# Attention of the picked rows in a graph and feed-forward network: context products in two halves, the mix's last rows added tile by tile

## The reference, cut to what matters

```
normed = _ln(hidden_states, g1, b1)
scores = sigmoid(normed @ Wr + br)
_, idx = top_k(-scores, k)                    # k = 188 rows of 1250 are picked
q, kk, v = normed @ Wq + bq, normed @ Wk + bk, normed @ Wv + bv     # 12 heads of 64
probs = softmax(q @ kk^T / sqrt(64))
ctx = probs @ v
attn_out = ctx @ Wo + bo
pooled = sum(w * normed)                      # w = scores / (sum(scores) + 1e-6)
mix_out = (normed + scores * pooled) @ Wm + bm
merged = where(picked, attn_out, mix_out)
h = hidden_states + merged
n2 = _ln(h, g2, b2)
return h + gelu(n2 @ W1 + bf1) @ W2 + bf2
```

## Time and profile before

| what | value |
| --- | --- |
| time, median of 3 runs | 3018.88 us |
| lowest and highest | 3018.45 and 3022.26 us |
| the profiled execution's own time | 3013.21 us |
| its span | 3011.5 us |
| PE busy | 2577.1 us (86%) |
| PEld busy | 2053.6 us (68%) |
| DVE busy | 2083.0 us (69%) |
| ACT busy | 1282.9 us (43%) |
| POOL busy | 313.8 us (10%) |
| mean granted clock of PE | 0.913 |

### The profile page before, as it was taken

How to read it: one execution, slowest core, us unless ns; L and a number is a source line. 1 busy time by engine, 2 the same in 40 slices (tenths; PEclk the granted TensorE clock), 3 DMA queues, 4 the chain that set the end, 5 groups by cost and what they waited for, 6 DMA issues and landing times. The chain is left out here.

```text
span 3011.5 us, 36877 instructions
## 1 busy us (share of the span) xinstructions
PE 2577.1 (86%) x13464; PEld 2053.6 (68%) x13465; DVE 2083.0 (69%) x3004; ACT 1282.9 (43%) x1560; POOL 313.8 (10%) x160
## 2 busy tenths in 40 slices
PE   7887894888854994799999999699999989897989
PEld 3556891323322994455699999599888769896768
DVE  6775899999963554599288889560467688235655
ACT  1573226988920000111477777222565563222511
POOL 0000000000003895000000000251000000000013
PEclk9997556999975997899999999899999999998989
DMA  2467443511005554542555643362534352312003
GB/s 68 135 181 174 149 144 114 194 35 51 17 32 160 199 194 133 211 173 95 162 162 169 179 117 106 111 198 79 179 120 130 99 180 94 84 48 64 1 26 93
DMA packets 165812, 366.01 MB, mean 122 GB/s; under 512 B 29390, under 2 KB 89628, under 8 KB 164769
## 3 DMA queue, kind: packets, MB, share of 16 engines
q1 hardware_dynamic: 120728, 274.54, 30.3%
q10 hardware_dynamic: 35968, 73.97, 6.9%
q0 software_dynamic: 8960, 15.41, 2.0%
HBM read 280.88 MB, written 82.93 MB: 121 GB/s over the span
## 5 line engine op out<-in xcount | busy, mean ns | idle before, releaser
L1593 PE MATMUL gat_acc<-far_u,gat_ft 125*65 125x512 f32 x720 | 286.8, 539 | 57.7 <-DVE far_u L1661 57.3
L1593 PEld LDWEIGHTS gat_acc<-far_u,gat_ft 125*65 125x65 f32 x720 | 93.9, 142 | 246.9 <-issue 154.2
L1053 PE MATMUL rg_out<-rg_w,rg_hT 128*125 128x384 f32 x720 | 234.3, 489 | 0.0
L2183 PE MATMUL rg2a_acc<-rg2a_value_part,rg2a_wts_part 125*125 125x512 f32 x600 | 205.0, 342 | 14.8 <-DVE rg2a_wts_part L1902 11.4
L2184 PE MATMUL rg2a_acc<-rg2a_value_part,rg2a_wts_part 125*125 125x512 f32 x600 | 205.6, 343 | 0.0
L2185 PE MATMUL rg2a_acc<-rg2a_value_part,rg2a_wts_part 125*125 125x512 f32 x600 | 204.1, 340 | 0.0
L1053 PEld LDWEIGHTS rg_out<-rg_w,rg_hT 128*125 128x125 f32 x720 | 135.7, 189 | 97.5 <-issue 1.8
L1628 ACT ACTIVATE far_u<-gat_rows,gat_ks 125x1250 f32<-125x1250 f32 x118 | 156.8, 1329 | 43.1 <-PE gat_acc L1593 34.1
L1641 DVE TENSOR_TENSOR far_u<-far_u,gat_lowb 125x1250 f32<-125x1250 f32 x120 | 174.4, 1454 | 0.4 <-PEq L701 0.4
L1661 DVE SCALAR_TENSOR_TENSOR far_u<-far_u,counts_u 125x1250 f32<-125x1250 f32 x120 | 174.4, 1454 | 0.0
L370 PE MATMUL sums<-src_hot,key_hot 125*125 125x512 bf16 (+1 forms) x618 | 139.4, 355 | 27.0 <-DVE key_hot L305 25.5
(11 more groups left out here) (530 smaller groups left out, 6434.1 us busy)
## 6 DMA issues: line engine op xcount, KB each, us to landing
rg2a_values<-values_dram SPq DMA_DIRECT2D x89, 384.0 KB, 3.3
rg1a_counts<-counts_dram SPq DMA_DIRECT2D x26, 820.3 KB
rg_mask<-far_dram SPq DMA_DIRECT2D x60, 312.5 KB, 3.6
moe_raw<-in_L_ffn_w SPq DMA_DIRECT2D x16, 1152.0 KB, 5.7
relw_chunk<-in_L_gnn_W ACTq DMA_DIRECT2D x36, 384.0 KB, 3.1
gat_rows<-rows_dram SPq DMA_DIRECT2D x10, 1250.0 KB, 5.7
sorted_dram<-gat_zeros SPq DMA_DIRECT2D x30, 384.0 KB, 9.0
values_dram<-rg_stage ACTq DMA_DIRECT2D x30, 384.0 KB, 2.3
```

The lines of the kernel that those rows point to most:

```text
L1053: last = pe.matmul(self.out_ps[n % 2][:, a, 0:384], self.hT[:, c, t * TP:(t + 1) * TP], self.w_sb[r % 2][:, c, a * 384:(a + 1) * 384], sta ...
L1593: last = pe.matmul(acc[h % 2][0:WIDTH, b, 0:c1 - c0], ft[:, t, h, :], wts[i % HB][:, c0:c1], start=(t == 0), stop=(t == NT - 1))
L2183: pe.matmul(out, still[0], moving[0], start=first, stop=False)
```

## The change

Three things are moved, and no arithmetic is added or removed.

1. `context(i)` becomes two halves of five products. PE's order for a pair is now turn, half a context, turn, half a context, and so on. The waits of the context stay ahead of its first half, its signal `ctx_made` behind the second.
2. The four bias products with `bo` are taken ahead: two before the last unit's context, two behind it. The wait for DVE's last taking of a context stands behind them.
3. In the third mix piece the rows are added tile by tile: from tile 5 on, behind the taking of each product, the rows of two tiles are added. The first two pieces stay as they were.

```diff
@@ keys_and_mix, DVE
-            def add_rows(m):
+            def both_parts(m):
 
                 dve.wait_ge(row_in, 32 * (m + 1))
+                link(dve.tensor_tensor(extra[0:TP, 0, :], extra[0:TP, 0, :], extra[0:TP, 1, :], op=ALU.add))
+
+            def add_rows(m, t):
+
                 cols = slice(m * PIECE, (m + 1) * PIECE)
-                link(dve.tensor_tensor(extra[0:TP, 0, :], extra[0:TP, 0, :], extra[0:TP, 1, :], op=ALU.add))
-                for t in range(NT):
-                    link(dve.scalar_tensor_tensor(out=z[:, t, cols], in0=extra[0:TP, 0, :], scalar=keep[:, 1, t:t + 1],
-                                                  in1=z[:, t, cols], op0=ALU.mult, op1=ALU.add))
-                    last = dve.scalar_tensor_tensor(out=z[:, t, cols], in0=extra[0:TP, 2, :], scalar=keep[:, 0, t:t + 1],
-                                                    in1=z[:, t, cols], op0=ALU.mult, op1=ALU.add)
-                last.then_inc(row_used, 1)
+                link(dve.scalar_tensor_tensor(out=z[:, t, cols], in0=extra[0:TP, 0, :], scalar=keep[:, 1, t:t + 1],
+                                              in1=z[:, t, cols], op0=ALU.mult, op1=ALU.add))
+                return dve.scalar_tensor_tensor(out=z[:, t, cols], in0=extra[0:TP, 2, :], scalar=keep[:, 0, t:t + 1],
+                                                in1=z[:, t, cols], op0=ALU.mult, op1=ALU.add)
...
-                if t == NT - 1:
-                    dve.wait_ge(dve_took, n + 1)
-                    add_rows(m)
+                if m < PIECES - 1:
+                    if t == NT - 1:
+                        dve.wait_ge(dve_took, n + 1)
+                        both_parts(m)
+                        for u in range(NT):
+                            last = add_rows(m, u)
+                        last.then_inc(row_used, 1)
+                elif t >= 5:
+                    if t == 5:
+                        both_parts(m)
+                    for u in (2 * t - 10, 2 * t - 9):
+                        dve.wait_ge(dve_took, n - t + u + 1)
+                        last = add_rows(m, u)
+                    if t == NT - 1:
+                        last.then_inc(row_used, 1)
@@ attend_picked, PE
-            def context(i):
+            def context(i, half):
                 q, h = units[i]
                 at = slice(h % 2 * DH, h % 2 * DH + DH)
-                pe.wait_ge(turned_out, 2 * i + 2)
-                if i:
-                    pe.wait_ge(ctx_out, i)
-                for t in range(NT):
+                if half == 0:
+                    pe.wait_ge(turned_out, 2 * i + 2)
+                    if i:
+                        pe.wait_ge(ctx_out, i)
+                for t in range(5 * half, 5 * half + 5):
                     last = pe.matmul(ctx_ps[at, 0:QT], v[:, t, h * DH:(h + 1) * DH],
                                      probsT[i % 2][:, t, :], start=(t == 0), stop=(t == NT - 1))
-                last.then_inc(ctx_made, 1)
+                if half == 1:
+                    last.then_inc(ctx_made, 1)
+
+            def bias(q):
+                for a in range(2):
+                    cols = slice(a * 384, (a + 1) * 384)
+                    pe.matmul(score_ps[q][0:QT, a, 0:384], ones[:, :], bo_row[:, cols], start=True, stop=False)
 
             scores(0)
             for i in range(len(units)):
                 if i % 2 == 0 and i + 2 < len(units):
                     scores(i // 2 + 1)
-                turn(i, 0)
-                if i:
-                    context(i - 1)
-                turn(i, 1)
-            context(len(units) - 1)
-            pe.wait_ge(ctx_out, len(units))
+                for half in range(2):
+                    turn(i, half)
+                    if i:
+                        context(i - 1, half)
             pe.wait_ge(wo_in, 16)
             pe.wait_ge(small_in, 32)
             pe.wait_ge(one_set, 1)
+            bias(0)
+            for half in range(2):
+                context(len(units) - 1, half)
+            bias(1)
+            pe.wait_ge(ctx_out, len(units))
             for q in range(2):
                 for a in range(2):
                     cols = slice(a * 384, (a + 1) * 384)
-                    pe.matmul(score_ps[q][0:QT, a, 0:384], ones[:, :], bo_row[:, cols], start=True, stop=False)
                     for c in range(KC):
```

## The result

The changed kernel is slower. Over 20 runs each, its median is 3043.01 us (3021.61 to 3054.99) against 3019.59 (3014.77 to 3025.45); the ratio is 1.0073, 95% interval 1.0058 to 1.0089. On the 3018.88 of the prediction that ratio makes 3040.9, inside the range of 3021 to 3042 near its upper end; the bare median lies 1 us above it. The direction and the mechanisms were as forecast. The size was +22 us by the ratio in place of +12.6.

The account below looks back on a forecast made before the run. The prediction took the chain through DVE and ACT, as long as PE's 9.50 us period, as the bound. Terms -5.8 - 1.0 + 14.5 - 1.1 + 6.0 = +12.6 on 3013.21 gave 3025.8, plus 5.7 to the median: 3031.5, range 3021 to 3042.

Parts of the forecast that it names:

- What bounds the kernel: Loop over pairs: the chain through PE, DVE and ACT is as long as the 9.50 us period, without slack.
- Mix, -5.8: End of the mix: ACT's copy at 2740.72 becomes last, against 2746.54, -5.8 us; bound -4.6 with rows landing late.
- First scores, -1.0: First scores after the mix: shorter idleness may keep the clock up; bounds 0 and -2.1 us, middle taken.
- Loop, +14.5: Loop over pairs: half a turn 0.71 and half a context 0.90 join the chain, period 11.11, nine periods +14.5 us.
- Last pair and end, -1.1: Last pair to end of the products with Wo: -1.1 us, of which early biases filling two waits give 1.07.
- Clock, +6.0: Loop: PE idles some 1.8 us in one piece, clock falls in four of ten pairs, 1.5 us each.
- The faster one: Rival, loop: taking a context doesn't hold the second maximum, halves fill 0.74 us per pair; 3003 us, chance 0.08.
- No falls of the clock, 3025.5: Rival, loop: it lengthens but the clock stays up, 3018.88 + 6.6 us; chance 0.25.

Follow-up runs that it names:

- e3: Changed kernel with DVE's taking of the context moved behind the pair's second maximum; 3006.25 us, ratio to before 0.9946.
- e8: Changed kernel with ACT's two exponentials of a pair one copy later, DVE's order left; 3001.44 us, ratio to before 0.9941.
- e9: Changed kernel profiled once more, nothing altered; 3035.55 us (one).
- e5: Changed kernel with four unread products more per pair in PE's idle piece before turn(a+1, 1); 3027.79 us, ratio to before 1.0023.
- e4: Changed kernel with DVE's taking behind the second maximum and ACT's two exponentials of a pair one copy later; 3000.17 us, ratio to before 0.9933.
- e1: Changed kernel with the contexts whole again between the two turns; 3007.95 us, ratio to before 0.9956.
- e2: Kernel before with the contexts in halves and nothing else; 3054.31 us, ratio to before 1.0106.
- e6: Kernel before with only the third mix piece's rows added tile by tile; 3013.39 us, ratio to before 0.9983.
- e10: Kernel before profiled once more, nothing altered; 3026.15 us (one).
- e11: e4 with two unread products more in PE's wait ahead of the spreading stage; 3001.09 us, ratio to before 0.9926.

## Why the prediction was right, and where it was off

In the first pair of profiles the sum is +17.8 against the forecast +12.6. Of the 5.2 between them the clock makes 4.7 and the loop 1.8; the first scores and the end came out 1.4 better.

**What bounds the kernel.** Right. The chain scores, turn, context, taking, second maximum, exponential, copy, turn was the period, without slack. e3 and e8 cut it at two different links, and the period fell to 9.36 and 9.19.

**Mix, -5.8.** Right: the gap before the first scores fell from 7.96 to 2.10, 5.9 us, with the rows landing 0.23 us late, which ACT's copy hides. The bound of -4.6 doesn't follow from its rows: 2725.88 + 4.3 + 9.71 + 1.65 = 2741.54 against 2746.54 makes -5.0. Nothing hung on it.

**First scores, -1.0.** Between the bounds, as a mean of two outcomes: 2.1 in five of nine profiles, 0.6 to 0.7 in four. The gap of two microseconds keeps the clock up in some executions and not in others.

**Loop, +14.5.** Right in mechanism, 1.8 us short: 11.31 in place of 11.11 per period, 16.3 in nine. The step that was off is the half context, which I took as 0.90, half of the whole. Five products take 0.96 between turns. All three half contexts of a period that lie on the chain cost that 0.06 more: 0.17 of the 0.20.

**Last pair and end, -1.1.** The biases give 2.05 by themselves, because products of one kind in a row run shorter than those between others, which the rows of before did not show. The changed kernel's profile has 40.08 against 39.91 all the same. 1.7 us of that are the sixth fall, the scores of its last pair (4.04 in place of 2.34), and belong to the clock; the other 0.5 are the lengthened chain. Without the fall the stretch is 1.5 us shorter, near the forecast.

**Clock, +6.0.** This term was mis-sized, and it is the greatest part of the miss. I had four falls in ten pairs, 1.5 us each. The changed kernel's first profile has six, 1.6 to 1.7 each, 9.9 us in all, and another 0.84 left over from the pairs before the loop. That of e9 has seven: six in the nine periods, five of 1.6 to 1.7 and one of 2.8 (28.44 - 16.3 - 1.0 left over = 11.1), and a seventh from which the clock came back only in the products with Wo, which cost another 11 us; the forecast had nothing of that kind. So the number of falls was off more than their price. The price I had taken from the unit that stood beside a fall in the earlier trace rows, a turn and a context; in the loop it is mostly the scores of the next pair that pay, 3.5 to 4.0 us in place of 2.34. The case itself, that an idle piece of 1.8 us among short products lets the clock fall, was right, and e5 shows cause and price: the piece filled, the clock stays and 15 us come back. Why it falls behind some of these pieces and not behind others stays open.

**The rivals.** The faster one fell: the second maximum is held by the taking. It was right on one point that I had not seen as a kernel: with the taking and the exponentials out of the way, e4, the halves do fill the waits. That e4's 3000 is close to that rival's 3003 is partly luck: the ten loop pairs were to give 7.4 us and the end 2, and in e4's profile nine periods give 3.45 and the end 3.66. No falls of the clock, 3025.5: refuted by both profiles, and nearly what e5 measures with its filler (3027.79). By the Trainium skill (TensorE: Matmul & The Clock Gate, section Why this matters for your kernels) nothing should have fallen in the loop, since no idle gap in it was as long as those it warns of; the trace disagrees, with falls behind gaps of 1.88 us, so the measurement decides.

**What stays open.** The start of the first scores lies between 2732.9 and 2750.9 us in the thirteen profiles, for reasons ahead of the change, of which the mix part explains 6. That spread of executions is seen and not explained here. That medians differ by more than the first pair of profiles does is in keeping with e9, but two profiles don't give a distribution. The other way round, in e1, e3, e4 and e8 the medians gain 2 to 7 us more than the stages of their one profile add up to (e8: 11.5 by stages, 18 measured). That is not explained either, so the stages carry the argument and the medians only its direction and rough size.

## What to carry to other kernels

Before filling an idle gap of an engine, follow the wait that the filler delays. Here 0.74 us of idleness was off the chain, and the half turn put ahead of a context's last product was on it, through two other engines. When a product is moved back, look at what its consumer's engine has queued behind the consumer: a copy out that stood between two maxima, and an exponential that stood ahead of a copy, carried the 0.7 us of half a turn to PE's next turn, and with the half context ahead of the next scores, 0.96, the pair became 1.81 us longer. The same halves gave 0.55 us per pair (9.50 to 8.95) as soon as those two queues were reordered, which costs a line each. And count the clock when a wait among short products grows: behind 1.88 us of it the clock fell in six and in seven of ten pairs.

## What the runs showed of the hardware that I had not expected

The low clock can last through work without a pause. In six of twelve profiles without a filler there (e1, e2, e3, e5, e6, e10) the clock fell behind the 2.03 us wait ahead of the spreading stage and stayed at 0.50 through eighty products, though PE had no idle time in them. From e1, windows, and the row of PE:

```profile
2886.00:2890.00 4.00, 3.37 (x12) 0.64 0.02 4
2900.00:2910.00 10.00, 10.00 (x33) 0.50 0.00 0
...
2886.63 25.59 PE L3359 MATMUL att_score<-att_out,picksT 94*125 94x384 f32 x80 [2.04 <-DVE att_out L3403]
```

In the other six the same products behind the same wait took 16.5 us with the clock up. A fall there costs 8 to 9 us, in part of the executions, whether or not the kernel has the change: before has 16.50 and, in e10, 25.40; e4, e8 and both profiles of the changed kernel have 16.5, e1, e3 and e5, made from it, 24 to 26. What decides it is not shown; e11's filler was to settle it and did not.
